# Two attention layers on one core: where the two groups of score matmuls stand in a unit's slot

## What is computed

```python
xn = layernorm(x, g_in)
q = (xn @ Wq).reshape(b, n, H, DH).transpose(0, 2, 1, 3) * scale
kv = xn @ Wkv
k, v = (kv[..., :DH], kv[..., DH:])
...
sim = jnp.einsum('bhid,bjd->bhij', q, k)
sim = sim + bias
sim = jnp.where(causal_mask, neg, sim)
sim = jnp.where(mask_p[:, None, None, :], sim, neg)
attn = jax.nn.softmax(sim, axis=-1)
out = jnp.einsum('bhij,bjd->bhid', attn, v)
out = out.transpose(0, 2, 1, 3).reshape(b, n, INNER)
out = out @ Wo
return layernorm(out, g_out)
...
x = x + _L0_cond_ref(x, ...)
x = x + _L1_cond_ref(x, ...)
```

## Time and profile before

| | |
|---|---|
| median of 3 runs | 2149.84 us (2149.3 to 2150.18) |
| the profiled execution | 2148.31 us, of it the span of its instructions 2146.5 us |
| busy: TensorE, VectorE, ScalarE, GpSimd | 97%, 75%, 72%, 48% of the span |
| granted TensorE clock, mean | 0.989 of full speed |

### The profile page before, as it was taken

One profiled execution on the slowest core, in us unless ns is written; L12 is line 12 of the kernel. 1 busy time (PEld: TensorE's weight loads), 2 busy tenths in 40 slices (PEclk: granted clock), 3 DMA queues, 4 the chain that ended last, 5 costly groups with the idle time before them and its releaser, 6 DMA issues.

```text
span 2146.5 us, 72068 instructions
## 1 busy us (share of the span) xinstructions
PE 2081.1 (97%) x26363; PEld 1858.4 (87%) x26363; DVE 1601.2 (75%) x3422; ACT 1554.9 (72%) x6241; POOL 1028.4 (48%) x1510
## 2 busy tenths in 40 slices
PE   5899999999999999999999999999999999999987
PEld 4788988988988988988988988888988888888876
DVE  5777777777777777777777777777777777777765
ACT  4667777777777777777777777777777777777775
POOL 3444544544544544544544544544544554544543
PEclk8999999999999999999999999999999999999998
DMA  8112222212222212222222222212222212222221
GB/s 267 49 54 60 75 63 63 70 58 61 75 63 63 70 57 62 75 63 63 70 57 62 75 63 63 70 57 62 75 63 63 70 57 63 75 63 62 63 57 42
DMA packets 183034, 147.47 MB, mean 69 GB/s; under 512 B 121440, under 2 KB 125616, under 8 KB 182992
## 3 DMA queue, kind: packets, MB, share of 16 engines
q1 hardware_dynamic: 181248, 145.77, 22.7%
q0 software_dynamic: 688, 1.14, 0.3%
q10 hardware_dynamic: 1056, 0.00, 0.0%
HBM read 98.56 MB, written 37.77 MB: 64 GB/s over the span
## 4 chain that ended last, share of the span: by engine, by line
PE 91%; POOL 2%; ACT 2%; DVE 2%; SPq 2%; issue 1%; DMA 1%; POOLq 0%; DVEq 0%; ACTq 0%
PE psum L709 32%; PE psum L615 18%; PE psum L581 16%; PE psum L692 8%; PE psum L674 8%; PE psum L543 3%; PE psum L632 3%; PE psum L592 2%; ACT o_hi L907 1%; SPq L386 1%; POOL probs L1475 1%; POOL masked_bias L1465 1%; ACT probs L901 1%; DMA xa<-in_x_dram 1%; PE psum L623 0%
## 5 line engine op out<-in xcount | busy, mean ns | idle before, releaser
L901 ACT ACTIVATE probs<-probs,neg_max 128x129 f32<-128x129 f32 (+3 forms) x2048 | 712.4, 351 | 58.2 <-DVE neg_max L1141 58.1
L1465 POOL TENSOR_TENSOR masked_bias<-bias,pad_neg 128x516 f32<-128x516 f32 (+3 forms) x512 | 399.3, 813 | 205.8 <-DVE probs L1135 199.8
L1475 POOL TENSOR_TENSOR probs<-probs,den_inv 128x512 f32<-128x512 f32 (+3 forms) x512 | 368.0, 740 | 172.5 <-DVE den_inv L1146 172.5
L1487 POOL TENSOR_TENSOR y_out<-y_out,res 128x512 f32<-128x512 f32 x128 | 165.5, 1293 | 526.7 <-ACT y_out L865 526.7
L901 ACT ACTIVATION_READ_ACCUMULATOR probs<-probs,neg_max 128x1 f32 x2048 | 385.9, 188 | 0.0
L1151 DVE STREAM_TRANSPOSE probs_t<-probs 128x512 f32<-128x512 f32 (+3 forms) x512 | 229.9, 487 | 196.8 <-POOL probs L1475 195.7
L1135 DVE TENSOR_TENSOR probs<-psum,masked_bias 128x648 f32<-128x648 f32 x256 | 212.8, 831 | 112.5 <-PE psum L674 109.0
L709 PE MATMUL psum<-wo_hi,o_hi 128*128 128x512 f32 x1024 | 272.7, 409 | 9.2 <-ACT o_hi L907 7.4
L907 ACT ACTIVATE o_hi<-psum,null_v_col 128x512 fp32r<-128x512 f32 x256 | 161.9, 683 | 155.5 <-PE psum L692 155.5
L709 PE MATMUL psum<-wo_hi,o_lo 128*128 128x512 f32 x1024 | 262.9, 398 | 0.1
L709 PE MATMUL psum<-wo_lo,o_hi 128*128 128x512 f32 x1024 | 260.6, 396 | 0.0
(11 more groups left out here) (133 smaller groups left out, 3910.6 us busy)
## 6 DMA issues: line engine op xcount, KB each, us to landing
res<-in_x_dram SPq DMA_DIRECT2D x64, 256.0 KB, 2.6
v_rep<-v_kept SPq DMA_DIRECT2D x512, 32.0 KB, 1.8
x_of<-y_out SPq DMA_DIRECT2D x64, 256.0 KB, 2.1
res<-x_of SPq DMA_DIRECT2D x64, 256.0 KB, 2.7
out_dram<-y_out SPq DMA_DIRECT2D x64, 256.0 KB, 2.1
xa<-in_x_dram SPq DMA_DIRECT2D x63, 256.0 KB, 2.7
xa<-x_of SPq DMA_DIRECT2D x63, 256.0 KB, 2.7
q_aside<-qp SPq DMA_DIRECT2D x32, 256.0 KB, 3.0
```

The costliest lines, as they stand in the source:

```text
L901: x_ = nc.scalar.activation(s, s, ACT.Exp, bias=neg_max[:, b, n:n + 1], accum_out=den[:, b, n:n + 1])
L1465: m = nc.gpsimd.tensor_tensor(block(masked_bias, b), block(bias[u.layer], b), pad_neg[u.layer][:, 0:WIDTH[b]].unsqueeze(1).to_broadcast([P ...
L1475: m = nc.gpsimd.tensor_tensor(some, some, den_inv[:, b, :].unsqueeze(2).to_broadcast([P, 4, n]), ALU.mult)
```

## The change

At the end of a slot, all values of the present unit come first, and then both score groups of the next unit, one straight after the other; nothing of them is left for the head of the next slot. VectorE adds the bias to both groups at the end of a slot. The addition for group 0 is split into one instruction for each of its two PSUM banks, each with a semaphore of its own (`bank_read[e]`). TensorE waits for bank 3 before the transpositions of the input and for bank 2 before `project_out`; the bank that the next slot needs first is read first: (1, 0) ahead of a slot that begins with transpositions, (0, 1) ahead of one that begins with `project_out`. In `first`, VectorE's `row_max(u, 1)` moves behind `split_x(w.even)`. The scores of unit 1 of layer 0, like those of unit 0, use 64x128 tiles and half as many matmuls. GpSimd waits for `biased`, the addition for group 1, as before. The same edits are made in the start-up functions, which are left out here.

```diff
             def transpose_even(w, u):
                 if u:
-                    wait(pe, biased[0], u.done)
+                    wait(pe, bank_read[1], u.done)
                 transpose_x(w.even)
...
                 if p == 0:
                     wait(pe, y_taken, u.prev)
                     if now:
-                        wait(pe, biased[0], now.done)
+                        wait(pe, bank_read[0], now.done)
...
-                tr = P if static(u, 0, 0) else TR
+                tr = P if static(u, 0, 0) or static(u, 0, 1) else TR
...
             def first(u, v, w, n, then):
-                scores(u, 1)
                 transpose_even(w, u)
                 project_out(v, 0, u)
                 project_out(v, 1)
                 transpose_odd(w)
                 project_out(v, 2)
                 project_pair(w, 0, (0, 1, 2, 3), u)
+                values(u, range(BLOCKS))
                 scores(then, 0)
-                values(u, range(BLOCKS))
+                scores(then, 1)
 
             def second(u, v, w, n, then):
-                scores(u, 1)
...
                 project_pair(w, 1, (3,), u)
-                scores(then, 0)
                 wait(pe, pair_v_ready, w.pdone * 2)
                 values(u, range(BLOCKS))
+                scores(then, 0)
+                scores(then, 1)
 
             def late(u, v, w, n, loads, then, pairs_done):
-                if u:
-                    scores(u, 1)
...
-                    values(u, range(2))
+                    values(u, range(BLOCKS))
                 if then:
                     scores(then, 0)
-                if u:
-                    values(u, range(2, BLOCKS))
+                    scores(then, 1)
...
-            def add_bias(u, c):
-                if c == 0:
-                    for g in range(len(GROUPS)):
-                        wait(dve, turned[g], u.prev)
-                    wait(dve, masked_bias_done, u.done)
-                wait(dve, scores_done[c], u.done)
-                nc.vector.tensor_tensor(pairs(probs, c), SB[c][:, :, 0:ROW], pairs(masked_bias, c), ALU.add).then_inc(biased[c], 1)
+            def add_bias(u, banks):
+                for g in range(len(GROUPS)):
+                    wait(dve, turned[g], u.prev)
+                wait(dve, masked_bias_done, u.done)
+                wait(dve, scores_done[0], u.done)
+                for e in banks:
+                    nc.vector.tensor_tensor(probs[:, e, :], SB[0][:, e, 0:ROW], masked_bias[:, e, :], ALU.add).then_inc(bank_read[e], 1)
+                wait(dve, scores_done[1], u.done)
+                nc.vector.tensor_tensor(pairs(probs, 1), SB[1][:, :, 0:ROW], pairs(masked_bias, 1), ALU.add).then_inc(biased, 1)
...
             def first(u, v, w, n, then):
                 input_statistics(w.odd)
-                add_bias(u, 1)
                 row_max(u, 3)
                 normalise(w.odd)
+                split_x(w.even)
                 row_max(u, 1)
-                split_x(w.even)
                 split_o(v, 0)
...
                 turn(u, 1)
                 normalise(n)
-                add_bias(then, 0)
+                add_bias(then, (1, 0))
 
             def second(u, v, w, n, then):
-                add_bias(u, 1)
...
-                add_bias(then, 0)
+                add_bias(then, (1, 0))
 
             def late(u, v, w, n, loads, then, pairs_done):
                 if u:
-                    add_bias(u, 1)
...
-                    add_bias(then, 0)
+                    add_bias(then, (1, 0) if n else (0, 1))
```

More of the change, by code:

```diff
@@ L326, in build @@
         scores_done = [sem(f"scores_done{n}") for n in range(2)]
-        biased = [sem(f"biased{n}") for n in range(2)]
+        biased = sem("biased")
+        bank_read = [sem(f"bank_read{e}") for e in range(2)]
         max_done = [sem(f"max_done{b}") for b in range(BLOCKS)]
@@ L565, in project_pair @@
                         if u:
-                            wait(pe, biased[1], u.done)
+                            wait(pe, biased, u.done)
                         elif h == 1:
@@ L729, in transpose_diagonals @@
                 pe.wait_ge(dve_step, vector_step("diagonals"))
-                pe.wait_ge(biased[0], u.done)
+                pe.wait_ge(bank_read[1], u.done)
                 nc.tensor.transpose(DIAG[0:H, 0:S], diag_sb[:, :], ident[:, :]).then_inc(pe_step, 1)
@@ L1127, in take_kt @@
                 nc.vector.tensor_scalar(keys[:, 1:1 + S], Q[2][:, 0:S], k_scale[:, 0:1], None, ALU.mult).then_inc(keys_ready, 1)
-            def add_bias(u, c):
-                if c == 0:
-                    for g in range(len(GROUPS)):
-                        wait(dve, turned[g], u.prev)
-                    wait(dve, masked_bias_done, u.done)
-                wait(dve, scores_done[c], u.done)
-                nc.vector.tensor_tensor(pairs(probs, c), SB[c][:, :, 0:ROW], pairs(masked_bias, c), ALU.add).then_inc(biased[c], 1)
+            def add_bias(u, banks):
[7 more added lines that the diff above has]
+                nc.vector.tensor_tensor(pairs(probs, 1), SB[1][:, :, 0:ROW], pairs(masked_bias, 1), ALU.add).then_inc(biased, 1)
             def row_max(u, b):
                 if b == 3:
-                    for c in range(2):
-                        wait(dve, biased[c], u.done)
+                    for e in range(2):
+                        wait(dve, bank_read[e], u.done)
+                    wait(dve, biased, u.done)
                 nc.vector.tensor_reduce(neg_max[:, b, :], block(probs, b), AX.X, ALU.max, negate=True).then_inc(max_done[b], 1)
```

9 lines of the change are left out of this document (4 added, 5 removed).

## The result

The changed kernel takes 2172.08 us (median of 4 runs, 2171.11 to 2174.14), the kernel before beside it 2150.01 us (4 runs). The ratio is 1.0104, with a 95% interval of 1.0092 to 1.0116: the change costs 22 us, where I had forecast 3 and a range up to 2168. The profiled execution took 2171.11 us, its span 2169.3 us against 2146.5.

A forecast was written before the change was run, and what follows sets the result against it. TensorE bounds the kernel, running groups back to back. Boundaries -0.75 and "first" +0.88 make +0.13 us a round, +4 over 30 rounds, -1 behind the loop: 2151.3 profiled, 2152.8 us as median; range 2138 to 2168.

The forecast's parts named there:

- The chain of "first": Slot "first": later input statistics delay row maximum, xn, o_lo, exponentials and last transposition, so the slot grows by 0.88 us.
- S: Start of the next slot after the change, put at 1.49 us after the start of the first score group.
- xn and GpSimd's mask collide: In "first", xn falls inside the mask's first piece on a shared port and ends at S+3.69, 0.90 us later.
- ScalarE's wait for the maximum of block 1: In "first", the maximum ends at about S+4.62, ScalarE is ready at S+4.37: another 0.28 us.
- the boundary: End of every slot: from start of values to next slot 2.83 us, being 1.34 to scores plus 1.49 to S.
- the second: Rival: each slot's first instruction waits on bank_read beyond T+1.49, four times a round; 2159 or 2182 us, chance 0.26.
- a missed turn of xn: In "first", xn waits behind a second piece of the mask: 0.76 us more, 2182 us with the late bank.
- The gain: Boundaries outside "first": -0.41 us in late before "second", -0.31 in the other late, -0.03 in "second"; -0.75 a round.
- 2131 us: By the tiling rule alone: fewer drains of TensorE in all four slots, -0.6 us a round.

The follow-up runs named there:

- the best kernel: Changed kernel with TensorE's old order in all slots but the late one before "second", odd unit's statistics between the additions again: 2137.92 us, 0.9950 of the kernel before.

## Why the prediction was wrong

**The chain of "first" was right.** The step that ends in "TensorE starts values at S+13.20" gave +0.88 us with a boundary of 2.83; the start of values was measured at S+13.21. Its parts were less exact: the row maximum at S+1.97 instead of S+2.08, xn's end at S+3.50 instead of S+3.69, the third pass of the output at S+5.14 instead of S+5.34, ScalarE's copy of y at S+8.95 instead of S+9.13, the last transposition at S+12.96 instead of S+13.14. That S+13.21 comes out in spite of it is partly luck: between the last transposition and the values there are 0.25 us where I had 0.06. The experiments bear out that this chain binds (12.41 us with early statistics) and that xn and GpSimd's mask collide (13.00 us with the mask behind xn). The Trainium skill (SBUF — State Buffer, "Who interferes with whom") calls the port pair that the two engines share an exclusive lock, under which the one that comes second fully blocks; the 0.38 us on xn and 0.19 on the mask agree with that. Not borne out is the 0.28 us that I gave to ScalarE's wait for the maximum of block 1: moving it changed nothing, since the next block's maximum, behind o_lo, is the later link.

**The step that failed is the boundary**, "from the start of values to S it is then 1.34 + 1.49 = 2.83 us in every slot". It was mis-sized by 0.11 to 0.26 us in each of four slots, 0.70 us a round and 21 us in all, which is the miss: 2153 and 19 make 2172. Taken apart by the rows:

- From values to the first score group I took 1.34 us from the earlier trace rows, and gave it no bounds. It was 1.36, 1.59, 1.35 (1060.07 to 1061.42) and 1.40 us. In "first" and "second" the waits of score group 0 used to stand behind the long matmuls of the projections; now they stand behind 64 short ones. With them moved in "first", 1.34 came back. I had said that these waits "stand ahead of groups that now run later than or where they did": right, none of them waited for anything, and all the same they cost up to 0.25 us.
- From the first score group to the bank's addition I took 0.95 us, midway; it was 0.99, 0.95, 0.99 and 0.98 us. Of the two rows that I stood between, the one with 1.00 was the better.
- The addition itself was estimated well, at 0.48 us for a measured 0.49 (0.90 for two).
- From its end to TensorE I took 0.06 us from the one row at start-up, and gave it no bounds either. It was 0.14, 0.06, 0.11 and 0.14 us. What makes it longer in three of the four is open.

The rival that came nearest is the second, the boundary that turns into a wait: its place was right, and that it decides from 0.01 us up. Its price of 2159 stood only on the 1.00 us, the one of 2182 on a missed turn of xn that did not occur, and its share, 0.26, was too small. For the sum of a term that is taken four times in a round and thirty rounds, 0.1 us is 12 us; so the two links that I had from one row each should have had a range from 0 to 0.2 us, and the whole range should have reached some 25 us higher.

**The gain was where I had it, and smaller.** The late slot before "second" was to win 0.41 us; it won 0.28 in the changed kernel and 0.30 alone, and this carries the best kernel: 30 rounds of 0.3 us are 9 of its 11 us. The other late slot was to win 0.31 us and won 0.18, but with its new order go the late statistics, which cost "first" 0.6. The page on tiling of the Trainium skill (TensorEngine Tiling (Array Packing), "Key Properties") has every change of tiling mode drain TensorE, and by it alone I had worked out 2131 us. The trace of before agrees that such a change costs something: its values in two pieces take 0.94 and 0.52 us to the score groups behind them (1047.46 to 1048.40, 1049.15 to 1049.67), in one piece 1.35. The changed kernel has fewer such changes, and still it is slower: where TensorE waits for a bank's read in any case, the time spared ahead of it was not seen again.

## What to carry to other kernels

Two matmul groups side by side spare a change of tile shape, but the group that stood between them was also the cover for the read of the first one's bank and for the chain on the other engines: ask of each group that is moved what it hid, in every slot by itself, and move it only where nothing was hidden. A term that comes back four times in each of thirty rounds needs its bounds to a tenth of a microsecond, with every link (issue, signal, handling of waits) ranged by more than one row. Where a kernel has slots of several kinds, try the new order in one kind at a time: here one of the four gained 0.28 us, and the other three together lost 1.10.

## What the runs showed of the hardware that I had not expected

- Waits that are long fulfilled were not free on TensorE where they stood behind short matmuls. With five of them between 64 small value matmuls and the scores the gap was 1.59 us and with four 1.40; with three it was 1.35 or 1.36, hardly more than the 1.34 to 1.36 with none. That the queue runs empty behind short matmuls is my reading of it; what the runs show is the gap, and that it goes when the waits are moved. Whether it is their number that counts is not shown: the fifth is always the one for the queries set aside.
- The same five waits cost nothing in the round that is written out behind the loop, where the values they compare with are constants and not taken from registers: there the gap in "first" is 1.35 us, in the same kernel. The loop also has a semaphore increment ahead of the scores, but that stayed in place when the waits were moved and the gap fell to 1.34.

```profile
2024.34 1.42 PE L693 MATMUL psum<-probs_t,v_rep 32*64 32x256 f32 x64
2025.69 0.32 PE L675 MATMUL psum<-kv_t,q_aside 64*64 64x129 f32 x1
```

- From the end of a VectorE instruction to the matmul that waits for it there were 0.06 to 0.14 us at the banks and 0.25 us at probs_t (1043.16 to 1043.41), where four waits stand at the head of the values.
